# Causal attention with scores made transposed, kept in an SBUF ring until the row maximum is known

## The reference

```python
def layernorm(x): return (x - mean(x)) / sqrt(var(x) + 1e-5)      # rows of 256
x = y_all                                   # (2, 2048, 256) float32
n = layernorm(x)
q = (n @ Wq + bq) / sqrt(256);  k = n @ Wk + bk;  v = n @ Wv + bv
w = softmax(where(causal, q @ k.T, -inf))   # per batch, 2048 x 2048
x = x + (w @ v) @ Wo + bo
h = layernorm(x);  p = h shifted down one row (zeros first)
r = sigmoid((mu_r*h + (1-mu_r)*p) @ W_r.T)
a = square(relu((mu_k*h + (1-mu_k)*p) @ W_k.T))
x = x + r * (a @ W_v.T)
```

## Time and profile before

| | us |
|---|---|
| runs | 404.18, 406.23, 407.58; median 406.23 |
| profiled execution, span from first to last instruction | 404.5 |
| TensorE busy | 381.2 (94%) |
| VectorE busy | 306.3 (76%) |
| ScalarE busy | 226.2 (56%) |
| GpSimd busy | 141.3 (35%) |

### The profile page before, as it was taken

One profiled execution on the slowest core, in us unless ns is written; L12 is line 12 of the kernel. 1 busy time (PEld: TensorE's weight loads), 2 busy tenths in 40 slices (PEclk: granted clock), 3 DMA queues, 4 the chain that ended last, 5 costly groups with the idle time before them and its releaser, 6 DMA issues.

```text
span 404.5 us, 7159 instructions
## 1 busy us (share of the span) xinstructions
PE 381.2 (94%) x2607; PEld 345.6 (85%) x2607; DVE 306.3 (76%) x808; ACT 226.2 (56%) x514; POOL 141.3 (35%) x186
## 2 busy tenths in 40 slices
PE   5879999899999999999989989999999889999966
PEld 4768998799989999899978979889998779898946
DVE  1688977997879966766899946987669966954763
ACT  2345467557575455762656666547448367556543
POOL 2053420542553241425322562535122520731630
PEclk9999999999999999999999999999999999999976
DMA  7700000000300002003000000020010000000100
GB/s 176 226 2 1 2 2 0 3 0 2 104 2 1 2 28 78 2 0 105 1 2 0 2 2 23 4 78 2 0 53 2 1 0 2 23 31 2 52 24 30
DMA packets 12034, 10.81 MB, mean 27 GB/s; under 512 B 1888, under 2 KB 12000, under 8 KB 12000
## 3 DMA queue, kind: packets, MB, share of 16 engines
q1 hardware_dynamic: 12000, 10.36, 8.5%
HBM read 6.17 MB, written 4.19 MB: 26 GB/s over the span
## 4 chain that ended last, share of the span: by engine, by line
PE 67%; DVE 24%; issue 4%; ACT 2%; DMA 1%; POOL 1%; SPq 0%; DVEq 0%
PE G L732 7%; PE G L736 7%; PE G L735 7%; PE S L735 6%; PE PT L861 6%; PE S L732 6%; PE S L736 6%; PE O L732 6%; PE O L736 6%; PE O L735 6%; DVE mix L646 4%; PE G L766 3%; DVE x_in L599 2%; DVE pT_lo L477 2%; DVE scratch L524 2%
## 5 line engine op out<-in xcount | busy, mean ns | idle before, releaser
L329 ACT ACTIVATE pT_hi<-PT 128x512 fp32r<-128x512 f32 (+2 forms) x80 | 42.5, 532 | 98.6 <-PE PT L861 98.5
L732 PE MATMUL O<-v_hi,pT_hi 128*128 128x256 f32 x272 | 79.5, 292 | 0.0
L736 PE MATMUL O<-v_hi,pT_lo 128*128 128x256 f32 x272 | 76.8, 283 | 0.0
L735 PE MATMUL O<-v_lo,pT_hi 128*128 128x256 f32 x272 | 76.7, 282 | 0.0
L373 ACT ACTIVATE prob<-prob,neg_max 128x512 f32<-128x512 f32 (+2 forms) x80 | 52.1, 651 | 18.5 <-DVE neg_max L578 18.5
L735 PE MATMUL S<-kT_lo,xT_hi 128*128 128x512 f32 (+2 forms) x160 | 61.3, 383 | 0.0
L732 PE MATMUL S<-kT_hi,xT_hi 128*128 128x512 f32 (+2 forms) x160 | 58.8, 368 | 0.0
L736 PE MATMUL S<-kT_hi,xT_lo 128*128 128x512 f32 (+2 forms) x160 | 58.3, 364 | 0.0
L288 POOL TENSOR_TENSOR mix_lo<-mix,mix_hi 128x512 fp32r<-128x512 f32 (+1 forms) x32 | 41.4, 1314 | 41.6 <-ACT mix_hi L329 41.6
L265 POOL TENSOR_SCALAR var_eps<-mean_var 128x1 f32<-128x1 f32 (+1 forms) x40 | 8.9, 224 | 134.3 <-DVE mean_var L626 97.1
L477 DVE TENSOR_TENSOR pT_lo<-PT,pT_hi 128x512 fp32r<-128x512 f32 (+2 forms) x80 | 47.8, 597 | 9.7 <-ACT pT_hi L329 9.6
(11 more groups left out here) (136 smaller groups left out, 953.4 us busy)
## 6 DMA issues: line engine op xcount, KB each, us to landing
x_in<-in_L_attn_y_all_dram SPq DMA_DIRECT2D x8, 512.0 KB, 5.0
out_dram<-gate SPq DMA_DIRECT2D x15, 256.0 KB, 2.1
h_row<-in_L_attn_Wk_dram SPq DMA_DIRECT2D x1, 256.0 KB, 2.8
h_row<-in_L_attn_Wq_dram SPq DMA_DIRECT2D x1, 256.0 KB, 3.0
o_sum<-in_L_attn_Wv_dram SPq DMA_DIRECT2D x1, 256.0 KB, 6.1
o_sum<-in_L_attn_Wo_dram SPq DMA_DIRECT2D x1, 256.0 KB, 6.3
mix<-in_L_ffn_W_k_dram SPq DMA_DIRECT2D x1, 256.0 KB, 4.2
mix<-in_L_ffn_W_r_dram SPq DMA_DIRECT2D x1, 256.0 KB, 4.5
```

Source lines behind the costliest of these rows:

```text
L329: a.activation(dst, src, ACT.Copy, **kw).then_inc(done, 1)
L732: mm(dst, a_hi, b_hi, start=n == 0, stop=False)
L735: mm(dst, a_hi, b_lo, start=False, stop=False)
L736: last = mm(dst, a_lo, b_hi, start=False, stop=end)
```

## The change

The scores are made transposed, keys on the partitions: step (J, j) is key tile j of 128 keys against all the queries of group J that see it (up to 512). Here J is one of nine groups, the last 512 rows in two halves of 256, so there are 94 steps. ScalarE (`keep_scores`) copies a step's scores with e, now a column and added as the bias, into a ring `st` of 16 tiles of 512 columns in SBUF. VectorE (`take_max`) keeps the elementwise maximum over key tiles in `peak`. When all steps of a group are made, TensorE transposes `peak` (`gather_peak`, "mt"), VectorE reduces it, TensorE spreads the result over the partitions (`spread_peak`, "mb") and ScalarE copies it to `peak_b`. Only then the weights are made from the ring: VectorE `shift` subtracts, ScalarE `exps` takes Exp and rounds to `p_hi`, GpSimd `weights_low` makes `p_lo`; three buffers. They are the stationary operand as they stand, without a transpose. v has a column of ones (258 columns in two of the three matmuls), which gives the row sum, and the four row tiles of a group add up in four PSUM banks over all key tiles, so `o_sum`, `alpha` and `row_sum` are gone. `act_hi`, `act_lo` now share the memory of `mix_hi`, `mix_lo`, with waits to match. All the tables are new, and which weighted sums stand in which slot is a table too (`PV_AT`); the weights of u stand one slot behind the weighted sum of u - 3.

```diff
+    GROUPS = [(G, 0, TG) for G in range(NG - 1)] + [(NG - 1, 0, TG // 2), (NG - 1, TG // 2, TG // 2)]
+    COUNT = [TG * (G % GB) + t0 + n for G, t0, n in GROUPS]
+    STEPS = [(J, j) for J in range(NJ) for j in range(COUNT[J])]
+    NR = 16
+    NP = 3
...
+    PV_AT = [7, 8, 10, 10, 14, 14, 14, 16, 16, 16, 18, 18, 28, 28, 28, 29, 29, 29, 30, 31, 31, 31, 33, 33, 40, 40, 40, 40, 40, 40, 40, 40, 40, 40, 41, 41, 41, 42, 42, 43, 46, 50, 52, 54, 56, 56, 56, 56, 61, 61, 61, 65, 72, 72, 74, 74, 77, 77, 77, 81, 81, 81, 83, 83, 83, 91, 91, 91, 94, 94, 94, 100, 102, 109, 116, 119, 132, 132, 132, 133, 133, 133, 136, 136, 136, 144, 144, 144, 149, 149, 149, 153, 160, 160]
+    MT_AT = [(4,), (11,), (24,), (40,), (43,), (52,), (66,), (78,), (95,)]
+    MB_AT = [(5,), (12,), (26,), (40,), (44,), (52,), (70,), (81,), (109,)]
...
+    P_AT = [max(PV_AT[u - NP] + 1 if u >= NP else 0, MB_AT[STEPS[u][0]][0] + 1) for u in range(NS)]
...
+            def weights_low(u):
+
+                r = cols_of(u)
+                pool.wait_ge(p_high, u + 1)
+                g.tensor_tensor(p_lo[:, u % NP, r], score_tile(u), p_hi[:, u % NP, r].bitcast(f32), ALU.subtract)\
+                    .then_inc(p_split, 1)
...
+            def keep_scores(s):
+
+                J, j = STEPS[s]
+                tile = (GROUPS[J][0] // GB) * GB * TG + j
+                n = PLACES[s][0]
+                sc.wait_ge(s_ready, s + 1)
+                if diagonal(s) >= 0:
+                    sc.wait_ge(dotted, tile + 1)
+                if n >= NR:
+                    sc.wait_ge(p_split, FILLED[n - NR] + 1)
+                a.activation(score_tile(s), bank_s[s % 2][:, cols_of(s)], ACT.Identity, bias=e_col[:, tile:tile + 1])\
+                    .then_inc(st_ready, 1)
...
+            def exps(u):
+                sc.wait_ge(sub_done, u + 1)
+                a.activation(score_tile(u), score_tile(u), ACT.Exp).then_inc(exp_done, 1)
+                sc.wait_ge(exp_done, u + 1)
+                if u >= NP:
+                    sc.wait_ge(pv_done, u - NP + 1)
+                high(p_hi[:, u % NP, cols_of(u)], score_tile(u), p_high)
...
             for s in SLOTS:
-                if 0 <= s + 1 < NS:
-                    pT_part(s + 1)
-                if s + 2 < NS:
-                    exps(s + 2)
+                for u in P_IN[s]:
+                    exps(u)
+                if 0 <= s < NS:
+                    keep_scores(s)
...
+            def take_max(s):
+
+                J, j = STEPS[s]
+                r = cols_of(s)
+                dve.wait_ge(st_ready, s + 1)
+                if j == 0:
+                    if J > 0:
+                        dve.wait_ge(mt_ready, J)
+                    v.tensor_copy(peak[:, r], score_tile(s)).then_inc(maxed, 1)
+                else:
+                    dve.wait_ge(maxed, s)
+                    v.tensor_tensor(peak[:, r], peak[:, r], score_tile(s), ALU.max).then_inc(maxed, 1)
...
+            def shift(u):
+                J = STEPS[u][0]
+                if u == FIRST[J]:
+                    dve.wait_ge(mb_done, J + 1)
+                v.tensor_tensor(score_tile(u), score_tile(u), peak_b[:, cols_of(u)], ALU.subtract).then_inc(sub_done, 1)
...
             for s in SLOTS:
-                if s + 2 < NS:
-                    scores(s + 2)
-                if diagonal(s - 2):
-                    h_part(s - 2)
-                if diagonal(s - 1):
-                    x1_part(s - 1)
-                if 0 <= s + 1 < NS:
-                    pT_part(s + 1)
+                for u in P_IN[s]:
+                    shift(u)
+                if 0 <= s < NS:
+                    take_max(s)
+                for u in DONE_IN.get(s - 2, ()):
+                    h_part(u)
+                for u in DONE_IN.get(s - 1, ()):
+                    x1_part(u)
...
+            def pv(u):
+                J, j = STEPS[u]
+                G, t0, n = GROUPS[J]
+                c0 = cols_of(u).start
+                pe.wait_ge(p_split, u + 1)
...
+                for i, q in enumerate(tiles_of(u)):
...
+                    mm(bank_o[q][:, 0:VW], p_hi[:, u % NP, w], v_hi[:, j, :], start=j == 0, stop=False)
+                    mm(bank_o[q][:, 0:C], p_hi[:, u % NP, w], v_lo[:, j, :], start=False, stop=False)
+                    last = mm(bank_o[q][:, 0:VW], p_lo[:, u % NP, w], v_hi[:, j, :], start=False, stop=end)
```

More of the change, by code:

```diff
@@ L43, in attention_channel_mix_block @@
+    LAST = NJ - 1
+    COUNT = [TG * (G % GB) + t0 + n for G, t0, n in GROUPS]
+    FIRST = [sum(COUNT[:J]) for J in range(NJ + 1)]
+    STEPS = [(J, j) for J in range(NJ) for j in range(COUNT[J])]
     NS = len(STEPS)
-    FIRST = [sum(TG * (g % GB + 1) for g in range(G)) for G in range(NG + 1)]
     def diagonal(s):
[L47 to L56, removed]
@@ L364, in exps @@
-            def exps(s):
-                G, c, p = STEPS[s]
-                w = width(s)
-                sc.wait_ge(s_used, s + 1)
-                total = row_sum[:, p:p + 1] if c == 0 else part_sum[:, c % 2, p:p + 1]
-                if c > 0:
-                    a.activation(alpha[:, c % 2, p:p + 1], neg_max[:, (c - 1) % 2, p:p + 1], ACT.Exp,
-                                 bias=neg_max[:, c % 2, p:p + 1], scale=-1.0)
-                a.activation(prob[:, s % 2, 0:w], prob[:, s % 2, 0:w], ACT.Exp, bias=neg_max[:, c % 2, p:p + 1], scale=-1.0,
-                             accum_out=total).then_inc(exp_done, 1)
@@ L435, in _ @@
             sc.wait_ge(fold_ready, 5)
[L436 to L437 removed]
+            high(wvo_hi[:], pairs(bank_o[0]), fold_moved)
             ffn_part(0)
@@ L848, in scores @@
                 bank, mask = bank_s[s % 2], None
-                if diagonal(s):
-                    if p == 0:
-                        pe.wait_ge(kT_split, KC * (G + 1))
-                    mask = (bank[:, rows], ident_b[:], mask_b[:])
-                product(bank[:, 0:keys.stop - keys.start],
-                        [(xT_hi[:, G % NT, k, rows], xT_lo[:, G % NT, k, rows], kT_hi[:, k, keys], kT_lo[:, k, keys])
-                         for k in range(KC)], mask).then_inc(s_ready, 1)
-            def pT(s):
-                pe.wait_ge(exp_done, s + 1)
-                for b in range(width(s) // P):
-                    last = nc.tensor.transpose(bank_p[s % 2][:, b * P:(b + 1) * P], prob[:, s % 2, b * P:(b + 1) * P], ident[:])
-                last.then_inc(pT_ready, 1)
@@ L864, in pv @@
-            def pv(s):
-                G, c, p = STEPS[s]
-                pe.wait_ge(pT_split, s + 1)
-                if s >= 2:
-                    pe.wait_ge(o_added, s - 1)
-                if diagonal(s) and p == 0:
-                    pe.wait_ge(v_split, 2 * (G + 1))
-                product(bank_o[s % 2][:, 0:C],
-                        [(pT_hi[:, s % 2, b * P:(b + 1) * P], pT_lo[:, s % 2, b * P:(b + 1) * P],
-                          v_hi[:, c * TG + b, :], v_lo[:, c * TG + b, :]) for b in range(width(s) // P)])\
-                    .then_inc(o_ready, 1)
@@ L878, in _, with gather_peak @@
-            pe.wait_ge(const_ready, 7)
+                if diagonal(s) >= t0:
+                    mask = (bank[:, r.start:r.start + P], ident_b[:], mask_b[:])
+                product(bank[:, left:r.stop],
+                        [(kT_hi[:, k, keys], kT_lo[:, k, keys], xT_hi[:, G % NT, k, q], xT_lo[:, G % NT, k, q])
+                         for k in range(KC)], mask).then_inc(s_ready, 1)
+            def gather_peak(J):
+                n = GROUPS[J][2]
+                free("mt", J, 0)
+                pe.wait_ge(maxed, FIRST[J + 1])
+                bank = bank_of("mt", J, 0)
+                for t in range(n):
+                    last = nc.tensor.transpose(bank[:, t * P:(t + 1) * P], peak[:, t * P:(t + 1) * P], ident[:])
+                last.then_inc(mt_ready, 1)
```

413 lines of the change are left out of this document (213 added, 200 removed).

## The result

The changed kernel takes 442.1 us (441.5 to 442.6) against 405.5 us of the kernel before on the same chip: ratio 1.090, 95% interval 1.086 to 1.094. The forecast was 399, its range 381 to 424.

The account below looks back on a forecast made before the run. TensorE's work was taken as the bound: its savings moved the end to 375.5 us, waits of 31 in place of 9.6 made it 396.9, and 1.7 for the median gave 398.6, so 399; range 381 to 424.

Parts of the forecast that it names:

- TensorE's part: TensorE's work over the steady part: transposes go, gathers and spreads come; 27.1 us less, first score step 1.9 us earlier.
- slot 40's wait: At J3's gather in slot 40, TensorE waits 5 to 6 us for the first weights; 8 us with GpSimd's pace.
- the sizes of the waits: TensorE's waits: start to slot 28 11 us, slot 40 8, middle 5, tail 7; sum 31 in place of 9.6.
- the tail: From slot 94 to the last weighted sum, GpSimd and its fill set the pace: 7 us of wait.
- four places: Start to slot 28, slot 40, middle (slots 44 to 63) and tail: where instruction order makes TensorE wait, 31 us.
- the 8 us before slot 28: TensorE's losses in the start, walked through from xT(1) to J2's first weights, small ones included; 8 us, without the lock.
- the lock term: Start to slot 28: two-SBUF-input VectorE passes wait for GpSimd, 0.22 us each, 9.5 us, of which 3 not hidden.
- the rival: Port waits make VectorE last in start and middle, GpSimd with it in the tail: waits 56 us, median 424; chance 0.22.
- the sign: VectorE busy above 85% between 28 us and the last weighted sum would show the prediction wrong.
- The third rival, the clock: TensorE's clock falls to half speed after gaps at slot 40 and in the tail: 402 to 409; with pacing 0.18.
- If the clock falls before 370: TensorE's granted clock falling before 370 us would show the prediction wrong.
- The last sign: ScalarE's keep_scores, not the matmuls, setting the distance between score steps would show the prediction wrong.

Follow-up runs that it names:

- The filler: 26 filler matmuls of 512 columns added on TensorE behind the spreads in slots 40, 44 and 52, against the changed kernel: 438.3 us, ratio 1.084.
- e8: Against the changed kernel, maximum taken one slot late and low halves written as zeros by GpSimd memsets (left out of the result): 409.05 us, ratio 1.007.
- e13: Against the changed kernel, maximum one slot late and low halves as longer memset series, 32 columns each (left out of the result): 412.15 us, ratio 1.015.
- e4: Against the changed kernel, maximum of each step taken one slot later, at once in a gather's slot; no instruction more or less: 423.1 us, ratio 1.045.

## Why the prediction was wrong

**TensorE's part was right.** First score step at 24.7 (25.7 predicted), O matmuls at 0.12 with 258 columns, 28 us of matmuls gone by start distances (27), the stretch behind the last weighted sum 21.4 us (21.5), ScalarE's prices, p_lo at 1.39 (1.29, and 1.40 as the upper price; half of the pair in the earlier trace rows is 1.28), slot 40's wait 5.6 us (5 to 6). TensorE's busy time was not: 374.6 us against about 350; it holds bars of 0.63 us at half speed where others have 0.39. Nor were the sizes of the waits: taking from each score step's start the matmuls ahead of it, the loss is 17 us up to slot 28 (11 predicted), 6 between 28 and 40 (none), 9.5 at slot 40 (8), 24 in slots 41 to 63 (5), 10 in 64 to 93 (none), 9 in the tail (7).

**The step that failed** is "No total reaches TensorE's 318. What counts is order, and there are four places". Order counts in many more places than four. The sentence on the start, "take_max(s) stands behind ScalarE's keep_scores(s), and this behind the exps of its slot", names the very link, and I priced it only as a part of the 8 us before slot 28. It holds in all 25 of the 94 slots that have weights to make, and the sum has nothing for it between slots 28 and 40 and behind 63. With one unit of 512 such a slot is a round of shift 1.04, exponential 0.62, rounding 0.63, copy 0.69, maximum 0.99, together 3.97 us and its handovers, each waiting for the one before. TensorE needs 6 x 0.23 + 12 x 0.12 = 2.8 us for the same step and unit, and 3.2 us per slot on average between slots 28 and 93 with all its other work. So in these slots the round, not TensorE, is last; that a total which stays below TensorE's says nothing about it is what I missed. That TensorE waits for this reason is shown by unlinking the maximum, which gave back 18 us, half of the loss: counted as above, 3 us of them up to slot 28, 6 between 28 and 40, 7 in 41 to 63, 6 in 64 to 93, and none at slot 40 and in the tail.

**The second is the lock term.** The collision, its condition and its place were right, and the rival had a chance of 0.22. "9.5 us here, of which I take 3 as not hidden" was the sizing: 0.22 per instruction against 0.36 and 0.31 in the groups view (1.0 when GpSimd never pauses), and less of it was hidden, since it lengthens two passes of the round above. Measured beside the late maximum: some 9 us for the ports, about 15 with p_lo's length. The rival's mechanism was right, its 424 too low, and its reason was incomplete: VectorE was busy 79% of 28 to 419 us (310.7 of 391), under the 85% that I had named as the sign. A busy share doesn't show an engine that is last in every round and waits in between.

**The third rival, the clock,** was there, with 27 us of half speed, 14 us short of a full clock. "If the clock falls before 370" was a sign that came true. The filler took away 2 of the 14 and gave back 2.6 us; the other 12 are an upper bound for what the clock still cost, and no run settles how much of it is real. The last sign did not come: TensorE's score matmuls waited 3.7 us in all for ScalarE's keep_scores.

**What stays open.** With both causes off, 409 stands against the 396 that my sum gives without its 3 us of lock. The windows of e8 lack 9 us to a full clock, so the clock can be a part of these 13, which no run took away. Most of the rest lies between slots 43 and 63, 17 us where 5 were predicted. In the timeline of e8 these are gathers that wait for the maximum and a feed-forward product that waits for a bank:

```profile
236.66 0.63 PE L848 MATMUL G<-ident,peak 128*128 128x128 f32 x4 [3.33 <-DVE peak L600]
...
280.01 0.80 PE L730 MATMUL G<-mix_hi,ffn_hi 128*128 128x512 f32 x1 [4.46 <-DVE xT_lo L502]
```

and ahead of the second, in the same view of VectorE and GpSimd, the feed-forward mix that was there before the change, with two SBUF inputs, beside mix_lo:

```profile
270.02 5.77 DVE L645 SCALAR_TENSOR_TENSOR mix<-hT,cols,mix 128x512 f32<-128x512 f32 x4
...
271.98 6.68 POOL L313 TENSOR_TENSOR mix_lo<-mix,mix_hi 128x512 fp32r<-128x512 f32 x4
```

Four mixes took 5.77 us where two that nothing delays take 1.40 in e13, so that four would take 2.8, and the scores' maximum and xT_lo stand behind them. That this part of the lock, which e8 doesn't remove, makes the wait of 4.46 is argued from these rows and was not tried.

## What to carry to other kernels

When work moves from the bounding engine to others, total times say little: write down the round that one slot makes through the in-order queues, with each handover, and compare that round with the bounding engine's time per slot. Then look for the link that needs no freshness; here the running maximum was wanted only at the gather, and taking it one slot late gave back half of the loss without changing an instruction. And where the same change keeps the neighbour busier, price a port collision above the mean of before: here that mean gave 0.22 us per pass, the changed kernel had 0.36 and 0.31, the shifts of slot 40 in e4 0.65, and back-to-back streams 1.0.

## What the hardware showed that I had not expected

VectorE and GpSimd instructions that collide don't add up fully: 0.61 and 1.22 us alone, 1.6 to 1.7 for a pair, not 1.83. VectorE is hit hardest in proportion: 2.6 times its time, GpSimd 1.4 times. GpSimd memsets of 64 columns in a row cost 0.087 us each, and VectorE's subtractions beside them kept their 0.61.
